# A mixture-of-experts kernel: a third row buffer for all batches, results sent ahead of rows, shorter pacing memsets and transposed logits

## What is computed

```python
# layer 1, per batch b: x (512 tokens, 512), f (512, 16), cond (512)
z = (x @ f / 512) @ f.T / 16
g = gelu(x @ W.T + fc_bias + z + cond)          # exact gelu
# layer 2, over all 8192 tokens
prob = softmax(g @ w_router + b_router)          # 16 experts
mask = top_k(prob, 4)
h = relu(g @ w1[e].T + b1[e])                    # 128 wide, expert e
y = sum over e of mask[e] * (h @ w2[e]) + b2
out = x + y
```

## Time and profile before

| | before |
|---|---|
| median of 3 runs | 1146.56 us (1144.09 to 1147.14) |
| the profiled execution: its time, its span | 1149.37 us, 1147.6 us |
| busy share of the span: PE, VectorE, ScalarE, GpSimd | 75%, 75%, 51%, 63% |
| stages 0 to 29, layer only | to about 173 us |
| stages 30 to 63, mixed | 173 to about 590 us |
| stages 64 to 101, experts only | 590 to about 934 us |
| sum phase | 934 us to the end |

### The profile page before, as it was taken

How to read it: one execution, slowest core, us unless ns; L and a number is a source line. 1 busy time by engine, 2 the same in 40 slices (tenths; PEclk the granted TensorE clock), 3 DMA queues, 4 the chain that set the end, 5 groups by cost and what they waited for, 6 DMA issues and landing times.

```text
span 1147.6 us, 18685 instructions
## 1 busy us (share of the span) xinstructions
PE 865.1 (75%) x4893; PEld 682.7 (59%) x4893; DVE 861.7 (75%) x2175; ACT 581.1 (51%) x1061; POOL 727.4 (63%) x1038
## 2 busy tenths in 40 slices
PE   8989989999999999999999876999999930000000
PEld 7757767777777776777777655788888820000000
DVE  4556666777687767767778974878998759987777
ACT  6535545756676575657657753766667610000000
POOL 1588888888888888888888897555555530000000
PEclk9989989999999999999999997999999965555555
DMA  6798679988899888988778887689987589999999
GB/s 188 262 330 299 236 270 334 310 293 298 288 314 305 289 285 300 312 282 297 265 276 313 302 289 262 245 296 342 317 282 243 192 313 425 425 427 429 426 432 378
DMA packets 103241, 354.88 MB, mean 309 GB/s; under 512 B 29961, under 2 KB 29961, under 8 KB 92384
## 3 DMA queue, kind: packets, MB, share of 16 engines
q1 hardware_dynamic: 59616, 217.22, 55.0%
q0 software_dynamic: 43424, 136.37, 30.3%
q10 hardware_dynamic: 96, 0.10, 0.0%
HBM read 200.47 MB, written 169.65 MB: 323 GB/s over the span
## 4 chain that ended last, share of the span: by engine, by line
PE 50%; DVE 14%; POOL 12%; DMA 11%; issue 7%; ACT 3%; another core or an unknown queue 2%; ACTq 0%; POOLq 0%; DVEq 0%; SPq 0%
PE lay L1185 12%; DMA w2l<-yt 9%; PE yps L1327 9%; PE hid L1294 8%; PE trn L1279 7%; POOL yt L563 4%; POOL xg L544 4%; PE hid L1299 4%; POOL w2l L528 3%; DVE stx L1040 3%; PE hid L1171 2%; PE trn L1206 2%; ACT gsb L643 2%; DMA outT<-ys 2%
## 5 line engine op out<-in xcount | busy, mean ns | idle before, releaser
L544 POOL DMA_INDIRECT xg<-grow,ix x224 | 226.7, 1012 | 70.2 <-issue 36.4
L817 DVE TENSOR_TENSOR gsb<-trn,gsb 128x512 fp32r<-128x512 f32 x239 | 162.4, 687 | 127.3 <-ACT gsb L643 75.2
L563 POOL DMA_INDIRECT yt<-ys,ids x170 | 176.7, 1039 | 72.6 <-issue 35.8
L1185 PE MATMUL lay<-w2l,xs 128*128 128x512 f32 x768 | 194.3, 403 | 0.0
L1279 PE MATMUL trn<-idf,gr 128*128 128x128 f32 x956 | 147.3, 277 | 27.0 <-DVE gsb L817 12.9
L1185 PEld LDWEIGHTS lay<-w2l,xs 128*128 128x128 f32 x768 | 144.6, 192 | 30.1
L528 POOL MEMSET w2l<- 128x320 f32 x412 | 161.3, 392 | 0.1
L1279 PEld LDWEIGHTS trn<-idf,gr 128*128 128x128 f32 x956 | 115.8, 142 | 68.3 <-DVE gsb L817 22.9
L643 ACT ACTIVATE gsb<-trn 128x512 fp32r<-128x512 f32 x239 | 142.6, 597 | 26.5 <-PE trn L1279 15.2
L1294 PE MATMUL hid<-gsb,w1c 128*128 128x512 f32 (+1 forms) x576 | 133.1, 374 | 11.9 <-ACT gsb L643 10.2
L671 ACT ACTIVATE hv<-hid,b1c 128x512 f32<-128x512 f32 (+1 forms) x94 | 52.6, 584 | 155.4 <-PE hid L1299 53.0
(11 more groups left out here) (243 smaller groups left out, 1823.9 us busy)
## 6 DMA issues: line engine op xcount, KB each, us to landing
gr<-xg SPq DMA_DIRECT2D x49, 1056.0 KB
xs<-yt SPq DMA_DIRECT2D x16, 2048.0 KB, 19.5
w2l<-yt SPq DMA_DIRECT2D x15, 2048.0 KB, 19.5
gr<-xg SPq DMA_DIRECT2D x45, 528.0 KB
stx<-xT SPq DMA_DIRECT2D x64, 256.0 KB, 4.3
outT<-ys SPq DMA_DIRECT2D x31, 512.0 KB, 20.4
xg<-xrow SPq DMA_DIRECT2D x16, 528.0 KB
w2f<-xrow SPq DMA_DIRECT2D x16, 512.0 KB
```

The source lines that it names most:

```text
L544: pool.indirect_dma_start(out=xg, out_offset=bass.IndirectOffsetOnAxis(ap=ix[:, row_buffer(b), q, k:k + 1], axis=0), in_=grows[row_buffer( ...
L563: pool.indirect_dma_start(out=yt, out_offset=bass.IndirectOffsetOnAxis(ap=ids[:, j % 8, c:c + 1], axis=0), in_=yss[result_buffer(j)][:, c, ...
L817: dve.tensor_tensor(gsb[:, :, LO, c * P:(c + 1) * P], turned[TURN_BANK[n]][:, :].rearrange("p (k t) -> p k t", k=KC), gsb[:, :, HI, c * P: ...
L1185: pe.matmul(lay[s % 2][:, :], xs[:, b % 2, k, h, cols], wls[:, k, a, :], start=(k == 0 and a == HI and h == HI), stop=False)
```

## The change

- Row buffers: three buffers in turn for all batches. The third is `grow3`, in the part of `w2l` of experts 11 to 14 (and the start of 15). `uw`, `zs` and `vw` move to experts 8 to 10.
- Result buffers: `yspare` is gone. A tile below 34 has one of two buffers; buffer 2 (the row buffer of batch 13) joins from tile 34 to 54, buffer 3 (`stx`) from 36 as before, buffer 4 from 39 to 54. Buffer 4 is `grow` 0 before and after, but its last rows are now those of batch 15, and were those of batch 14. So `result` of tile 39 waits for all rows of batch 15.
- Order on GpSimd: `place_rows` first up to iteration 32, `send` first in 33 to 66, `place_rows` first from 67 on.
- `rest` writes 160 elements in iterations below 32, 288 up to 63, 160 after. Its target is `fu` from iteration 69 on. `stop` is left out for the last three tiles.
- `presplit_w2` goes through the experts in order, two a stage, in stages 67 to 74 without a gap. Expert 15 waits for the memsets of iterations below 69, expert 11 for the rows of batch 14.
- Logits: four transposes against the identity `idf` take the place of four matmuls against `sumk`, which added the four partial sums over k. VectorE now adds them with a reduce of 256 inputs to 64 outputs, and takes the maximum from SBUF. The setup of `sumk` on GpSimd is gone.
- `b2` is loaded in stage 81 instead of 80, after all memsets.

```diff
@@ -29,14 +29,13 @@
-SPARE = 40
-MORE = 36, 39, 43, 55
+MORE = 34, 36, 39, 55
-REST = 320
+REST = 160, 288, 160
+DUMP = SLOTS + 5
-PRESPLIT = [*range(8), *range(12, NE), *range(8, 12)]
...
 def row_buffer(b):
-    return b % 3 if b < 6 else b % 2
+    return b % 3
...
     for j in range(NTILE):
-        free = [0, 1] + [2] * (j <= SPARE) + [3] * (j >= MORE[0])
-        free += [4] * (MORE[1] <= j < MORE[3]) + [5] * (MORE[2] <= j < MORE[3])
+        free = [0, 1] + [2] * (MORE[0] <= j < MORE[3]) + [3] * (j >= MORE[1]) + [4] * (MORE[2] <= j < MORE[3])
...
-        yspare = nc.alloc_sbuf_tensor_at("yspare", [P, 4, D], F32, offset=w2l_at + 8 * D * 4)
+        grow3 = nc.alloc_sbuf_tensor_at("grow3", [P, 4, W], F32, offset=w2l_at + 11 * D * 4)
...
-        yss = (ys[:, 0, :, :], ys[:, 1, :, :], yspare, stx, grow[:, 0, :, 0:D], grow[:, 1, :, 0:D])
+        yss = (ys[:, 0, :, :], ys[:, 1, :, :], grow[:, 1, :, 0:D], stx, grow[:, 0, :, 0:D])
...
                     pool.wait_ge(g_pace, paced[0])
-                idle = w2l[:, NE - 1, 0:REST].bitcast(F32) if s < SLOTS + 7 else rep[:, :, :].rearrange("p q e -> p (q e)")
+                if s == DUMP:
+                    pool.wait_ge(p_lt, NB)
+                n = REST[0] if s < LAG + 2 else REST[1] if s < SLOTS else REST[2]
+                idle = w2l[:, NE - 1, D - n:D].bitcast(F32) if s < DUMP else fu[:, 0:n]
...
-                elif c == 1:
+                elif c == 1 and j < NTILE - 3:
                     stop()
...
-                first = s <= LAG + 2 or q != 3
+                first = s <= LAG + 2 or SLOTS + 3 <= s
                 if 0 <= s - 7 < SLOTS and first:
...
-                elif result_buffer(j) > 3:
-                    b = NB - 6 + result_buffer(j)
+                elif result_buffer(j) > 1:
+                    b = NB - 5 + result_buffer(j)
                     for q in range(4):
                         act.wait_ge(s_sc[row_buffer(b)][q], rows_sent(b))
...
             def choose(b):
-                lgs = rps[:, 256:256 + 4 * NE].rearrange("p (q e) -> p q e", q=4)
+                lgs = lexp
                 dve.wait_ge(p_lt, b + 1)
-                step(dve.tensor_reduce(lmax[:, :], lgs, AX.X, ALU.max))
+                step(dve.tensor_reduce(lgs[:, :, :], rps[:, :].rearrange("p (q k e) -> p q e k", q=4, k=KC)[:, :, 0:NE, :],
+                                       AX.X, ALU.add))
+                step(dve.tensor_reduce(lmax[:, :], lgs[:, :, :], AX.X, ALU.max))
...
                 if e == NE - 1:
-                    dve.wait_ge(g_pace, 4 * SLOTS + 4 * (SLOTS + 5 - LAG))
-                if e == 8:
-                    dve.wait_ge(s_y[2], results_sent(max(j for j in range(NTILE) if result_buffer(j) == 2)))
+                    dve.wait_ge(g_pace, 4 * (DUMP - 7) + 4 * (DUMP - LAG - 2))
+                if e == 11:
+                    for q in range(4):
+                        dve.wait_ge(s_sc[2][q], rows_sent(NB - 2))
...
-                pe.wait_ge(g_s, KC + 1)
                 for q in range(4):
-                    last = pe.matmul(rps[:, 256 + q * NE:256 + (q + 1) * NE], lgT[:, q * P:(q + 1) * P], sumk[:, :],
-                                     start=True, stop=True)
+                    last = pe.transpose(rps[:, q * P:(q + 1) * P], lgT[:, q * P:(q + 1) * P], idf[:, :])
                 last.then_inc(p_lt, 1)
```

More of the change, by code:

```diff
@@ L109, in result_buffer @@
     return RESULT_BUFFER[j]
[L112 to L117, removed]
 def results_sent(j):
@@ L291, in adaln_ffn @@
         s_sc = [[sem(f"s_sc_{n}_{q}") for q in range(4)] for n in range(3)]
-        s_y = [sem(f"s_y_{n}") for n in range(6)]
+        s_y = [sem(f"s_y_{n}") for n in range(5)]
         s_yin = [sem(f"s_yin_{n}") for n in range(len(yin))]
@@ L297, in adaln_ffn @@
         s_gr = [sem(f"s_gr_{n}") for n in range(2)]
-        g_z, g_id, g_up, g_tok, g_k, g_s, g_pace = (
-            sem(n) for n in ("g_z", "g_id", "g_up", "g_tok", "g_k", "g_s", "g_pace"))
+        g_z, g_id, g_up, g_tok, g_k, g_pace = (
+            sem(n) for n in ("g_z", "g_id", "g_up", "g_tok", "g_k", "g_pace"))
         p_z, p_w, p_r, p_lt, p_rk, p_cnt, p_pos, p_tn, p_f1, p_y = (
@@ L375, in load_tile @@
                 for i in range(b + 1):
-                    if i + 3 > b or i == 5:
+                    if i + 3 > b:
                         for q in range(4):
@@ L426, in _ @@
                     store_tiles(b - 2)
-                if s == SLOTS + 16:
+                if s == SLOTS + 17:
+                    sp.wait_ge(g_pace, 4 * SLOTS + 4 * (PACED - LAG - 2))
                     sp.wait_ge(p_tn, TURN_BATCH[SLOTS - 1] + 1)
@@ L435, in _ @@
                 if s == SLOTS + 16 + 8:
-                    for n in (4, 5):
+                    for n in (2, 4):
                         sp.wait_ge(s_y[n], results_sent(max(i for i in range(NTILE) if result_buffer(i) == n)))
@@ L514, in _ @@
             pool.iota(order[:, :], [[1, 2]], base=0, channel_multiplier=2).then_inc(g_k, 1)
[L515 to L518, removed]
-                                   pattern=[[-1, NE]], channel_multiplier=1).then_inc(g_s, 1)
             paced = [0]
@@ L694, in result @@
                     act.wait_ge(p_r, SLOTS // 2)
-                elif result_buffer(j) > 3:
-                    b = NB - 6 + result_buffer(j)
+                elif result_buffer(j) > 1:
+                    b = NB - 5 + result_buffer(j)
                     for q in range(4):
                         act.wait_ge(s_sc[row_buffer(b)][q], rows_sent(b))
-                if j == 1:
-                    for q in range(4):
-                        act.wait_ge(s_sc[2][q], rows_sent(5))
                 act.activation(yss[result_buffer(j)][:, c, :], second_out[RESULT_BANK[4 * j + c]][:, :], ACT.Copy).then_inc(a_y, 1)
@@ L728, in _ @@
                     split_w2(j - 1, expert[j - 1][0])
-                for n in presplit_in(s):
-                    presplit_w2(PRESPLIT[n])
+                if SLOTS + 3 <= s < SLOTS + 3 + NE // 2:
+                    for e in range(2):
+                        presplit_w2(2 * (s - SLOTS - 3) + e)
                 if s == KC + 1 or q == 2 and 2 <= b <= NB:
@@ L1016, in result @@
                     dve.wait_ge(p_r, SLOTS // 2)
-                elif result_buffer(j) > 3:
-                    b = NB - 6 + result_buffer(j)
+                elif result_buffer(j) > 1:
+                    b = NB - 5 + result_buffer(j)
                     for q in range(4):
                         dve.wait_ge(s_sc[row_buffer(b)][q], rows_sent(b))
-                if j == 1 or (j == 0 and c == 3):
-                    for q in range(4):
-                        dve.wait_ge(s_sc[2][q], rows_sent(5))
                 dve.tensor_copy(yss[result_buffer(j)][:, c, :], second_out[RESULT_BANK[4 * j + c]][:, :]).then_inc(v_y, 1)
@@ L1125, in _ @@
                         take_tile(j + 1, c)
-                    if c % 2 == 0 and presplit_in(s):
-                        presplit_w2(presplit_in(s)[c // 2])
+                    if SLOTS + 3 <= s < SLOTS + 3 + NE // 2 and c % 2 == 0:
+                        presplit_w2(2 * (s - SLOTS - 3) + c // 2)
                     if s <= SLOTS and 0 <= j - 1 and c % 2 == 1 and c < chunks(j - 1):
```

16 lines of the change are left out of this document (7 added, 9 removed).

## The result

| | before | after |
|---|---|---|
| median of 4 runs | 1146.76 us (1144.09 to 1147.14) | 1180.11 us (1168.27 to 1189.35) |
| profiled execution: time, span | 1149.37, 1147.6 | 1189.35, 1187.5 |
| ratio | | 1.0262, interval 1.0171 to 1.0352 |

The change made the kernel 2.6% slower here. Forecast was 1141.5 us.

What follows compares the result with a forecast made beforehand. TensorE was taken to bound the mixed stages, GpSimd just fast enough. Terms -4.0 - 0.7 - 1.5 + 0.5 + 1.4 - 0.8 = -5.1 gave 1144.3 us profiled, 1141.5 us median; range 1126 to 1155.

Steps and rivals of the forecast that it cites:

- Shorter memsets: Less GpSimd time per memset: 0 in the first stages, -1.5 us in mixed stages, +0.5 us for competing DMA traffic.
- the lead is lost: GpSimd runs ahead before iteration 32, then must wait for TensorE's results, so 12.3 us less on GpSimd gain nothing.
- rival 2: Slower: 11.3 us of the break after stage 70 stay and the new wait comes on top: 1152.8 us; chance 20%.
- is not caused by GpSimd: TensorE's poor stretch from 700 us on, after the last rows landed: 11.3 us that may stay.
- TensorE bounds the mixed stages, and GpSimd is just fast enough: Mixed stages, 450 to 475 us: TensorE busy all 25.0 us; gelu waits for rows only 3.2 us in total.
- rival 1: The break shrinks (-4.4 us), or GpSimd held the mixed stages (-7 instead of -1.5): 1129.7 us; chance 25%.
- Contention of DMA: Rows sent earlier compete with loads of weights and x: +0.5 us taken, bounds 0 and +1.6.
- Logits: Transposes replace four matmuls: -4.0 us in mixed stages, -0.7 us in layer-only stages; bounds 0 and -8.
- The break: Stages 70 to 77: a 16 us ScalarE wait for batch 15's rows replaces old waits; 78.4 against 77.0 us, +1.4.
- the old break: Between stages 70 and 77 of the kernel before, waits for last rows and memsets: a loss of 16.1 us.
- a sign of being wrong: The prediction is wrong if ScalarE's forecast wait for rows in stage 70, 12 to 18 us, is missing.
- Third row buffer, order, `stop`: Row buffer: gelu's waits go, within the -1.5 us; results sent first: 0; `stop` omitted at the end: -0.8 us.

Runs made afterwards that it cites:

- e3: Kernel before with memsets of 160, 288 and 160 elements by stage, nothing else, calm chip: 1104.02 us, ratio 0.9742.
- e10: Kernel before with memsets of 160, 288 and 160 elements by stage, nothing else, late chip: 1182.99 us, ratio 1.0299.
- e14: Changed kernel with all memsets at 320 elements again, late chip: 1156.62 us, ratio 1.006.
- e4: Kernel before with transposed logits, nothing else, calm chip: 1135.26 us, ratio 1.0026.
- e5: Changed kernel with no edit, measured again on a calm chip: 1110.0 us, ratio 0.9816.
- e7: Changed kernel with result buffer 4 from tile 43 instead of 39, calm chip: 1098.24 us, ratio 0.9706.
- e17: Changed kernel with all memsets at 320 elements and result buffer 4 from tile 43, late chip: 1134.3 us, ratio 0.9886.
- e6: Kernel before with memsets of 160, 288 and 160 elements and transposed logits, calm chip: 1099.38 us, ratio 0.9728.
- e13: Kernel before with all memsets at 240 elements, late chip: 1222.2 us, ratio 1.0621.
- e11: Changed kernel with result buffer 4 from tile 43 and all memsets at 160 elements, late chip: 1200.06 us, ratio 1.0404.
- e9: Changed kernel with no edit, measured again on a late chip: 1176.36 us, ratio 1.0213.

## Why the prediction was wrong

- **The step that failed** is "Shorter memsets": "the lead is lost", worth 0 in the first stages and -1.5 in the mixed ones, -7 if GpSimd were the bound there, and beside it +0.5 for contention. In the prediction nothing but that contention could make short memsets cost. In its place, the pace that the memset sets decides on a late chip when TensorE's updates get through. Runs of the memsets alone showed -2.6% on a calm chip (e3) and +3.0% on a late one (e10), both far outside. With 320 elements the loss by quarter 32 is gone (e14, on another late chip: 194.5 us, after 228.6). Of the 39.9 us, 31.5 are in the stages that I priced at 0.
- **Why I missed the loss.** The trace of before had its signs: 78 late updates, and 63.9 us of waits for which the profile names no engine. The prediction doesn't mention them. The largest:

```profile
ACT hv L671 <- remote: 21.2, 6, 6.9
```

  The last of them, from 700 us on, stands in rival 2 as the part that "is not caused by GpSimd", because the last rows had landed. But GpSimd was still sending results, one DMA every 1.33 us up to 707.49, and of TensorE's updates three come 4.0 to 5.2 us late from 701.77 to 704.67 and five, 3.4 to 4.8 us late, in a burst from 710.38 to 710.60. How much of the 11.3 us they make was not tried.
- **Why I missed the gain.** "TensorE bounds the mixed stages, and GpSimd is just fast enough" fits late chips only. On calm ones GpSimd's period is the bound: gelu waits 68.0 us for rows in e4, the nearest to before of which there is a trace. That was rival 1, which I priced at -7 for the mixed stages; in the layer-only stages alone it is 14 us (183.3 against 197.0).
- **Contention of DMA** was not it. e5 has the DMA engines full in the early stages and loses nothing; two of its stretches:

```profile
50.00:75.00 25.00, 23.68 (x137) 17.27 (x136) 16.63 (x76) 14.40 (x26) 22.03 (x37) 1.00 1.02 372
110.00:135.00 25.00, 23.66 (x136) 17.26 (x135) 16.82 (x79) 14.26 (x25) 22.03 (x37) 1.00 0.77 261
```

  The Trainium skill, "DMA: Bandwidth & Descriptors", section "Issuing engines are not separate DMA queues", says that DMAs of all issuing engines run on the same 16 engines. The trace agrees with it as far as it goes, with rows, weights and x at a share of 1.02; the price that I took from it doesn't show.
- **Logits**: -4.7 forecast, -0.4% or 4 to 5 us measured twice on calm chips with the third row buffer; nothing or a small loss without it. The reading of the weight loads was right, though the earlier trace rows stand at 616 to 621 us, behind the mixed stages. By the formula for isolated matmuls of the Trainium skill, "TensorE: Matmul & The Clock Gate", section "Back-to-back issue gap", the edit would have cost 2.4 us; that is not borne out.
- **The break**: the wait of ScalarE for the last rows is there with the forecast size or more, 18.0 to 28.1 us against 16. On a calm chip stages 70 to 77 take 79.5 us with it (e5; forecast 78.4) and 63.4 without it (e7), and its price in the whole is 12 us. So rows that land early shrink the old break, and the wait for buffer 4 brought it back; with 320 elements it stays at 77.9 without that wait (e17). In the trace of after itself the wait is missing, which the prediction had named as a sign of being wrong: TensorE's updates are so late that rows had landed by the time `result` of tile 39 came up, and stages 70 to 77 take 61.8 us (713.6 to 775.4) against a forecast of 78.4.
- **Third row buffer, order, `stop`**: at most a few us together with short memsets on a calm chip (e7 to e6); `stop` was not tried alone.

What stays open: what GpSimd's indirect DMAs and TensorE's updates share that holds the latter up, and why two chips show none of it with the same kernel, the part of the recording included. That the memset's length makes the loss is shown (e10 beside before on one chip; e14 beside before on another, where 288 elements cost 2.4%); that GpSimd's beat sets when the updates come is shown by the phase and by the burst at its pauses. That the late updates are what the time is lost by rests on the waits that end with them; no run removes them and leaves GpSimd's pace. That it is the DMA and not the memset that blocks is argued, since longer memsets help. Whether 240 elements are worse than 160 (1.0621 in e13, 1.0404 in e11) is open too, since kernel and chip differ; so is a version for both kinds of chip, since e17 had no calm one. Part of the loss may be the clock: up to 900 us TensorE stood at its lower level (0.5 of the granted clock) for 89 us in after and 34 in before, in after mostly before 210 us and from 650 to 760, where it was partly idle; how much of the loss is the clock's own was not separated.

## What to carry to other kernels

Before pricing an edit of pace, add up the waits that the profile gives to no engine, and look at which engine's updates come late and whether they keep another engine's beat; a pause that looks idle may be what lets them through. Measure such a change on more than one chip: the same edit was worth -2.6% and +3.0%. And take a wait whose release is known (buffer 4) out of the schedule rather than hoping that others cover it; that was 1.1% for one number.

## What was unexpected of the hardware

- On three of five chips of the experiments, and in the first measurement, TensorE's semaphore updates come late while GpSimd issues indirect DMAs: up to 13.1 us at a period of 1.38 us (e9), up to 3.9 at 1.51 (before), and there mostly 0.65 or 1.40 us after a DMA's start. On one of the three it is seldom at 1.51 (9 in e17). On two chips none is late by 1 us at a period of 1.38.
- When GpSimd pauses they come in a burst, 0.05 to 0.1 us apart, 2.4 us after the last DMA's start in after.
- Of ScalarE's and VectorE's updates that the traces hold, none came over 0.51 us late beside them.
